# Attention followed by a deformable convolution: two dense taps by spans of rows, and attention scores in float32 by groups of 32 rows

## What is computed

```python
xn = group_norm(x)                                   # 32 groups
q, k, v = split(conv1x1(xn, qkv_w) + qkv_b)          # 4 heads of 32 channels
attn = softmax(q @ k.T * 32 ** -0.5)                 # 4096 x 4096 for each head and image
x = conv1x1(attn @ v, proj_w) + proj_b + x
feat_up = feat_s                                     # the resize keeps the size
om = conv3x3(conv1x1(concat(x, 2 * feat_up), W_off), W_om) + b_om
offset, mask = split(om); mask = sigmoid(mask)       # 8 groups x 9 taps at each pixel
for tap in 9: for group in 8:                        # 16 channels in a group
    val = bilinear(feat_up[group], y + tap_y + off_y, x + tap_x + off_x) * mask
    out += W_dcn[tap, group] @ val
out = relu(out + b_dcn) + x
```

## Time and profile before

| | us |
|---|---|
| median of 3 runs | 12816.8 (12783.6 to 12825.1) |
| the profiled execution | 12790.4 |
| its span | 12788.6 |
| busy in the span: TensorE | 8894 (70%) |
| VectorE | 7910 (62%) |
| ScalarE | 2914 (23%) |
| GpSimd | 10704 (84%) |
| mean granted TensorE clock | 0.819 |

### The profile page before, as it was taken

How to read it: one execution, slowest core, us unless ns; L and a number is a source line. 1 busy time by engine, 2 the same in 40 slices (tenths; PEclk the granted TensorE clock), 3 DMA queues, 4 the chain that set the end, 5 groups by cost and what they waited for, 6 DMA issues and landing times. The chain is left out here.

```text
span 12788.6 us, 126443 instructions
## 1 busy us (share of the span) xinstructions
PE 8894.0 (70%) x34036; PEld 3273.8 (26%) x34036; DVE 7910.4 (62%) x9169; ACT 2914.1 (23%) x3357; POOL 10703.5 (84%) x24581
## 2 busy tenths in 40 slices
PE   5666778765777767777666777766687766778732
PEld 1222222222222222222222222222232222222211
DVE  3466666666666666656666656666566666656633
ACT  2222222211222211222122222211222221222200
POOL 0488888887888888888788888888788888888888
PEclk8888888887888887888788888878788887888865
DMA  3222211112111111111211111111211111111111
GB/s 94 75 65 67 78 29 25 28 29 61 29 32 28 28 28 29 29 29 31 54 35 29 29 27 27 28 28 29 62 24 34 29 28 29 29 29 25 28 24 23
DMA packets 458806, 469.41 MB, mean 37 GB/s; under 512 B 150432, under 2 KB 274464, under 8 KB 458016
## 3 DMA queue, kind: packets, MB, share of 16 engines
q0 software_dynamic: 262144, 268.96, 10.3%
q1 hardware_dynamic: 97952, 119.95, 3.5%
q10 hardware_dynamic: 97920, 71.35, 1.8%
HBM read 390.46 MB, written 69.21 MB: 36 GB/s over the span
## 5 line engine op out<-in xcount | busy, mean ns | idle before, releaser
L408 POOL DMA_INDIRECT g<-patches,idx x8192 | 7862.1, 960 | 1254.6 <-issue 1180.1
L404 POOL TENSOR_TENSOR carrier<-carrier 128x1 f32<-128x1 f32 x15872 | 2766.3, 203 | 140.1
L982 DVE TENSOR_TENSOR ring<-ring,hats 128x1024 f32<-128x1024 f32 x1024 | 1259.3, 1230 | 2520.4 <-PE ring L655 2187.3
L494 ACT ACTIVATE p<-ring 128x1024 f32<-128x1024 f32 x2048 | 2089.2, 1022 | 2812.3 <-PE ring L622 1936.6
L597 PE MATMUL ring<-k,q 128*128 128x512 bf16 x4096 | 1763.9, 529 | 1216.2 <-DVE mx L844 796.3
L844 DVE TENSOR_REDUCE mx<-ring 128x1 f32<-128x1024 f32 x2048 | 2381.1, 1218 | 300.9 <-PE ring L597 300.9
L621 PE MATMUL ring<-q,k 128*128 128x512 bf16 x4096 | 1598.3, 390 | 307.3 <-ACT p L494 84.0
L622 PE MATMUL ring<-q,k 67*128 67x512 bf16 x4096 | 1584.9, 387 | 0.0
L655 PE MATMUL ring<-fx,hats 64*128 64x512 f32 x4096 | 1203.2, 666 | 230.8 <-ACT hats L482 178.8
L984 DVE TENSOR_REDUCE dval<-ring 128x16 f32<-128x1024 f32 x1024 | 1254.1, 1225 | 35.4
L678 PE MATMUL ps_a<-p,v 128*64 128x512 f32 x4096 | 1110.9, 621 | 2.0 <-ACT p L494 2.0
(11 more groups left out here) (117 smaller groups left out, 5707.2 us busy)
## 6 DMA issues: line engine op xcount, KB each, us to landing
g<-patches,idx POOLq DMA_INDIRECT x8192
patch_in<-in_fpad ACTq DMA_DIRECT2D x544, 64.0 KB
patches<-patch_out ACTq DMA_DIRECT2D x136, 256.0 KB
k<-k_parts SPq DMA_DIRECT2D x96, 256.0 KB
q<-q_parts SPq DMA_DIRECT2D x192, 128.0 KB
k_parts<-v SPq DMA_DIRECT2D x16, 768.0 KB
q_parts<-p SPq DMA_DIRECT2D x32, 384.0 KB, 2.6
p<-in_x SPq DMA_DIRECT2D x4, 2048.0 KB
```

Source lines behind the costliest of these rows:

```text
L404: last = nc.gpsimd.tensor_tensor(carrier[:, col:col + 1], carrier[:, 0:1], carrier[:, 0:1], ALU.add)
L408: nc.gpsimd.indirect_dma_start(out=g[:, part, j - CUTS[part] * GROUPS, :], out_offset=None, in_=patches[b], in_offset=bass.IndirectOffsetO ...
L494: nc.scalar.activation(p[:, n % 4, :, :], ring[u % 2][:, :, :], ACT.Exp, scale=SCALE)\
L982: then(V.tensor_tensor(cells, cells, hy[:, at * HEIGHT:(at + 1) * HEIGHT].unsqueeze(2).to_broadcast([128, HEIGHT, GC]), ALU.mult))
```

## The change

- **Scores.** Keys and queries stay float32 in SBUF (`kf`, `qf`, channels on the partitions), written by one ScalarE activation each; `k_parts`, `q_parts`, the splits and all their DMAs go. A head's score is one float32 matmul of 32 rows, at the head's own 32 rows of the array, and in the kt phase one bf16 matmul of 32 rows more, which subtracts the maxima (`ones_b` times `mq`).
- **Max phase.** Still 64 uses of 1024 columns, now two heads x 512 keys: two float32 matmuls of 32 rows on neighbouring row groups. VectorE reduces to two maxima at once.
- **Order in a kt.** Both pairs' float32 matmuls come first, then both pairs' bf16 matmuls, then (in even kt) `distances` and `blocks_of_set`, then `weigh` of the kt before.
- **Two dense taps.** `DENSE` is 2, so 7 taps are picked: 56 picks a tile, in parts of 16, 16, 16 and 8. The 16 dense (tap, group) units of a tile are done in 4 sets of 4. For a set, `distances` has 8 float32 matmuls; ScalarE makes the hats with 4 activations of 512 and 2 of 1024 columns; VectorE multiplies them (`weigh_hats`); `blocks_of_set` has 12 float32 matmuls of 128 rows and 208 columns, for 13 blocks of rows (a span of six rows each, two rows on the partitions, three pairs); VectorE takes the block that holds the pixel (`chosen`) by a multiplication and a sum over 832 results. A set is at kt 0, 2, 4 and 6 of a tile's eight, and its distances two kt earlier.
- `points` gets five more small operations on [128 x 16]. `fx` is loaded by 6 DMAs in place of 2. Sample parts write to their own columns of `g`.

```diff
-DENSE = 1
+DENSE = 2
 PICKED = TAPS - DENSE
-CUTS = tuple(min(2 * part, PICKED) for part in range(PARTS + 1))
+CUTS = tuple(min(2 * part, PICKED - (PARTS - part)) for part in range(PARTS + 1))
...
+SETS = 2 * DENSE
+SET_AT = tuple(i * KT_TILE // SETS for i in range(SETS))
+BLOCK = 5
...
+        def hats_before(t, i):
+            return t * KT_TILE + SET_AT[i - 1] if i > 0 else (t - 1) * KT_TILE + SET_AT[-1]
...
             def prepare(b):
...
-                    nc.scalar.activation(k_made[:, 0, :], ring[u % 2][:, :, :].rearrange("p i n -> p (i n)"), ACT.Identity,
-                                         bias=k_bias).then_inc(k_high, 1)
+                    nc.scalar.activation(kf[:, c * 1024:(c + 1) * 1024], ring[u % 2][:, :, :].rearrange("p i n -> p (i n)"), ACT.Identity,
+                                         bias=k_bias).then_inc(ring_free[u % 2], 1)
...
+            def make_hats(s, b, t, i):
...
+                nc.scalar.activation(made[:, 0, :], ring[k % 2][:, 0, :], ACT.Abs, bias=plus_x, scale=-1.0)
+                for pair in range(PAIRS):
+                    last = nc.scalar.activation(made[:, 1 + pair, :], ring[k % 2][:, 1, :], ACT.Abs, bias=pair_rows[:, pair:pair + 1],
+                                                scale=-1.0)
...
                             for i in range(2):
-                                last = mm(ring[u % 2][:, i, :], q1[:, h, sub * 128:(sub + 1) * 128], k1[:, h, lo:lo + 512],
+                                rows = slice((2 * pair + i) * HD, (2 * pair + i + 1) * HD)
+                                last = mm(ring[u % 2][:, i, :], qf[rows, sub * 128:(sub + 1) * 128], kf[rows, c * 512:(c + 1) * 512],
                                           start=True, stop=True)
...
+            def blocks_of_set(s, b, t, i, fresh):
+                k = set_use(s, t, i)
+                wait_slot_free(pe, before_att(s, b, k), k)
+                pe.wait_ge(hats_weighed, tile_number(s - 1, t) * SETS + i + 1)
...
+                    for pair in range(PAIRS):
+                        last = mm(cells, hats[:, i % 2, 1 + pair, j * 128:(j + 1) * 128], fx[:, pair, :, group * GC:(group + 1) * GC],
+                                  start=pair == 0, stop=pair == PAIRS - 1)
...
+            def scores(s, b, kt, fresh):
...
+                for pair in range(2):
+                    u = uses[pair]
+                    wait_slot_free(pe, before_att(s, b, u), u)
+                    for i in range(2):
+                        rows = slice((2 * pair + i) * HD, (2 * pair + i + 1) * HD)
+                        mm(ring[u % 2][:, i, :], kf[rows, n], qf[rows, :], start=True, stop=False)
+                for pair in range(2):
+                    u = uses[pair]
+                    for i in range(2):
+                        rows = slice((2 * pair + i) * HD, (2 * pair + i + 1) * HD)
+                        last = mm(ring[u % 2][:, i, :], ones_b[rows, :], mq[rows, :], start=False, stop=True)
                     last.then_inc(ring_full, 1)
...
+                for t, i in hats_at(s, kt):
+                    distances(s, b, t, i)
+                for t, i in sets_at(s, kt):
+                    blocks_of_set(s, b, t, i, fresh)
...
             def maxima(s, b, sub0, sub1):
-                        V.tensor_reduce(mx[:, n, c:c + 1], ring[u % 2][:, :, :], AX.XY, ALU.max).then_inc(ring_free[u % 2], 1)
+                        V.tensor_reduce(mx[:, n:n + 2, c], ring[u % 2][:, :, :], AX.X, ALU.max).then_inc(ring_free[u % 2], 1)
```

More of the change, by code:

```diff
@@ L408, in gather @@
                         nc.gpsimd.indirect_dma_start(
[L409 removed]
+                            out=g[:, j, :], out_offset=None, in_=patches[b],
                             in_offset=bass.IndirectOffsetOnAxis(ap=idx[:, t, j:j + 1], axis=0),
@@ new lines, in head @@
+                nc.scalar.activation(qf[:, :], ring[0][:, 0, :], ACT.Identity, bias=q_bias).then_inc(ring_free[0], 1)
+            def make_hats(s, b, t, i):
+                k = hat_use(s, t, i)
+                wait_slot_full(act, before_att(s, b, k), k)
+                made = hats[:, i % 2, :, :]
+                nc.scalar.activation(made[:, 0, :], ring[k % 2][:, 0, :], ACT.Abs, bias=plus_x, scale=-1.0)
+                for pair in range(PAIRS):
+                    last = nc.scalar.activation(made[:, 1 + pair, :], ring[k % 2][:, 1, :], ACT.Abs, bias=pair_rows[:, pair:pair + 1],
+                                                scale=-1.0)
+                last.then_inc(ring_free[k % 2], 1)
+                wait_slot_read(act, before_att(s, b, k), k)
+                for half in range(2):
+                    part = made[:, 2 * half:2 * half + 2, :].rearrange("p v n -> p (v n)")
+                    last = nc.scalar.activation(part, part, ACT.Relu, bias=ones_s[:, 0:1], scale=-1.0)
+                last.then_inc(hats_ready, 1)
@@ L535, in step @@
                     for t in dense_tiles(s):
-                        make_hats(s, b, t)
+                        for i in range(SETS):
+                            make_hats(s, b, t, i)
                         for part in range(PARTS):
@@ L611, in max_to_rows @@
                 for k in range(USE_M):
[L612 removed]
+                    u = max_use(s, k)
                     wait_slot_read(pe, before_att(s, b, u), u)
[L615 to L623 removed]
@@ L657, in columns_of_group @@
                 last.then_inc(ring_full, 1)
             def scores(s, b, kt, fresh):
-                t, j = divmod(kt, KT_TILE)
-                dense = t in dense_tiles(s)
-                if dense and j == 0:
-                    distances(s, b, t)
+                n = slice(kt * 128, (kt + 1) * 128)
+                uses = [score_use(s, kt, pair) for pair in range(2)]
                 for pair in range(2):
-                    scores_of_pair(s, b, kt, pair)
-                    if dense and pair < DENSE:
-                        columns_of_group(s, b, t, j, pair, fresh)
+                    u = uses[pair]
[3 more added lines that the diff above has]
+                        mm(ring[u % 2][:, i, :], kf[rows, n], qf[rows, :], start=True, stop=False)
@@ L756, in step @@
                     for t in dense_tiles(s):
-                        distances(s, b, t)
-                        for j in range(GROUPS):
-                            for d in range(DENSE):
-                                columns_of_group(s, b, t, j, d, fresh)
+                        for i in range(SETS):
+                            distances(s, b, t, i)
+                            blocks_of_set(s, b, t, i, fresh)
                         for part in range(PARTS):
@@ L781, in _ @@
             dve.wait_ge(consts_loaded, CONSTS)
-            V.tensor_scalar(minus_x[:, :], plus_x, -1.0, None, ALU.mult).then_inc(dve_setup, 1)
-            def split(then, src, bias, made, rest):
-                then(V.scalar_tensor_tensor(rest, src, bias, made[:, 0, :], ALU.add, ALU.subtract))
-                then(V.tensor_copy(made[:, 1, :], rest))
-                return V.tensor_sub(made[:, 2, :], rest, made[:, 1, :])
+            for pair in range(PAIRS):
+                V.tensor_scalar(pair_rows[:, pair:pair + 1], base_s[:, 4 * GROUPS:4 * GROUPS + 1], 2.0 * pair, None, ALU.add)
+            V.tensor_scalar(block_rows[:, :].rearrange("p (a b) -> p a b", b=2), steps_s[:, 0:STEPS_B, 0:SUB:2], BLOCK / 4.0, None, ALU.mult)\
+                .then_inc(dve_setup, 1)
+            dve.wait_ge(dve_setup, 2)
             def prepare(b):
@@ L1027, in step @@
                     for t in dense_tiles(s):
-                        for j in range(GROUPS):
-                            dense_group(s, b, t, j)
+                        for i in range(SETS):
+                            weigh_hats(s, b, t, i)
+                            dense_set(s, b, t, i)
                         for part in range(PARTS):
```

303 lines of the change are left out of this document (125 added, 178 removed).

## The result

| | before | after |
|---|---|---|
| median, us | 12820.0 (12783.6 to 12825.1, 4 runs) | 14463.2 (14460.4 to 14467.5, 4 runs) |
| span of the profiled execution | 12788.6 | 14462.1 |
| mean granted TensorE clock | 0.819 | 0.79 |

The ratio is 1.1289 (95% interval 1.1268 to 1.131). Forecast were 13610 us and a range of 12850 to 14600: slower was right and the time lies in the range, but the kernel lost 1643 us where the forecast has 790.

A forecast was written before the change was run, and what follows sets the result against it. GpSimd's picks bound the old kernel; then the TensorE, ScalarE and VectorE chain would, at 362 us plus 54 + 3 - 10 = 47 a step. Start, steps, image changes and tail: 57 + 292 + 1261 + 11452 + 114 + 430 = 13606, predicted 13610 (12850 to 14600).

The forecast's parts named there:

- +3 us for 64 uses: Max phase: a slot's loop gets about 0.05 us a use longer at 2.4 GHz, +3 us a step.
- the max phase stays at 1.2 GHz: Rival, max phase: a use takes 1.9 us in place of 1.2, +45 a step, about 15050 us; chance 0.10.
- From the last maximum to the last `weigh`, +54: Dense part of the kt phase: +49 us a step from kt pairs, +5 from parts of sampling; some 12 is work.
- the copies and the half part: VectorE's small edits: two copies for four, last sampling part with half the patches; put at 0, bounded by 3 us a step.
- The matmuls of four row groups: Kt scores: four float32 matmuls side by side in 0.95 us; with the bf16 ones 1.2 where 1.95 were.
- the set's 4.3 us: Kt phase, `blocks_of_set`: 24 instructions of 208 columns at 0.18 us each, 4.3 us a set.
- the wait ahead of the distances: Even kt: distances take the first pair's slot, free 1.3 us after the scores, following its exponential and a handoff.
- The rival with two row groups side by side: Rival, scores: only two row groups run side by side, 29 us a step more, 14500 us; chance 0.12.
- the faster one: Rival, kt phase: ring waits hidden, dense part adds 12 us a step in place of 54, 12310 us; chance 0.13.
- the waits at the ring: Kt phase: TensorE waits for slots that ScalarE or VectorE still reads; the +54 us a step beyond some 12 of work.
- The queries' trip, -10: Step's start: split queries' trips to HBM go, 11.2 us less 1.5 for the first use, -10 us a step.
- GpSimd's 331 us a step: GpSimd's picks: 224 a step at 1.478 us each, 331 us a step.

The follow-up runs named there:

- e2: Changed kernel with each max-phase matmul on 64 rows in place of 32 (two heads summed, so different maxima): 13599.3 us, ratio 1.062 to the kernel before.
- e3: Changed kernel with 4 block matmuls a set in place of 12, from one pair of rows: 13558.8 us in one run.
- e4: Changed kernel with `weigh` issued ahead of the next kt's distances and blocks: 14745.8 us in one run.
- e8: Changed kernel with zero-padded queries in the max phase, and fewer dense sets a tile in place of 4: three sets 12797.5 us, two sets 12936.7 us.

## Why the forecast fell short

The parts of a step in us, from the traces, for the chain that the forecast starts from (step 8 of before, 361.9 us), and step 14 of after and of e2:

| | before | after | e2 | change forecast | change in after |
|---|---|---|---|---|---|
| step's start to the first maximum | 14.4 | 5.8 | 5.8 | -10 | -9 |
| max phase, first to last maximum | 84.9 | 119.1 | 92.6 | +3 | +34 |
| last maximum to last `weigh` | 203.3 | 249.8 | 249.3 | +54 | +46.5 |
| last `weigh` to the next step | 59.4 | 58.8 | 58.7 | 0 | -1 |

- **The max phase: the step that failed.** The forecast took "+3 us for 64 uses" at 2.4 GHz. Measured are +34 us a step, at 1.71 us a use and 1.2 GHz against 1.16 to 1.18 before. The argument for 2.4 GHz was that TensorE would be busy without a break, from the offset convolution, whose matmuls cover all rows. TensorE was busy 96% and the clock stayed at 0.51. The forecast named the warning under the rival: half of the rows stand idle.
- **By the Trainium skill** ("TensorE: Matmul & The Clock Gate", part 1) the slow clock is the default and activity releases it. The forecast read activity as busy time. The runs say that with float32 matmuls on 32 of 128 rows, two at a time, busy time is not enough (0.51), and with 64 rows each the clock is 0.94.
- **The right rival** was "the max phase stays at 1.2 GHz", given 0.10. Its first reason, "it does so now", holds for the 16 us of the earlier trace rows and not for the phase (0.65 above); the second, the idle rows, is the one that e2 shows. It was priced at 15050 us from a use of 1.9 us, twice a stream of 0.95; at half the clock it is 1.71. With that, 0.51 over the forecast's use, it gives 13606 + 32 x 64 x 0.51 = 14650, with +36 us a step for the max phase where +34 are measured. The rest of the 190 us is mostly in the next bullet. What the clock alone is worth is less than 0.51 a use: in e2 a use takes 1.29 us on average, not 1.20, and the phase is 8 us longer than before and not 3.
- **From the last maximum to the last `weigh`, +54.** Measured are +46.5. From the first exponential on, 186.5 us became 241.0. Ahead of it, 16.8 us became 8.8: the first distances no longer stand there (6 us at a tile's start), two copies of the maxima take 0.42 us each where four took 2.50, and the part of sampling is half. The forecast put the copies and the half part at 0. The matmuls of four row groups, the set's 4.3 us and the wait ahead of the distances (1.18 us for 1.3) came as forecast. That the hats would be ready long before their use did not always hold: the blocks wait 139 us in all for `weigh_hats`. The rival with two row groups side by side (0.12) is out. So is the faster one: e3 and e4 show that the waits at the ring are real.
- **The queries' trip, -10.** Measured are -9.
- **The sum.** Start 52 for 57. Step 0: 330 for 292; e2 has 301, so 30 of these 38 are the clock's. Steps 1 to 3: 1374 for 1261; e2 has 1294, so 81 of 113. Steps 4 to 30: 11817 us where 27 x 409 + 114 = 11157 were forecast, 660 more, 27 x 24.4. Step 31 and the tail: 889 for 839. Together +856. In e2, with the clock put right, the same five terms are off by -7, +9, +33, -60 and +22. They add up to -3, so its match with the forecast is luck in part.
- **GpSimd's 331 us a step** were not the bound in after, as forecast, but they were too low: (14451.6 - 377.6 - 2854.1) / 7168 = 1.565 us a pick, 351 a step, reckoned as in the forecast from the rows of tile g. With fewer sets (e8) it mattered.

## What to carry to other kernels

Before small matmuls replace large ones, look at how many of the array's rows are fed at one time: a phase of them can stay at 1.2 GHz however busy it is (119 us here where 93 were possible). If rows stand idle anyway, feeding them zeros can be worth it (764 us here for four small activations a step). When an engine that was the bound gets work taken away, look first at what the others still do one after another at the phase borders; here three positions of 5.3 us stood on the path, and moving them, 12 us a step, made the difference between no gain and 2.6%.

## What the runs showed of the hardware that I had not expected

**The clock goes by more than TensorE's busy share.** Float32 matmuls of 512 columns in the max phase: 32 rows each on two row groups, busy 117 of 122 us, 0.51; 64 rows each, busy 79 of 95 us, 0.94; 64 rows each with half of the stationary rows zero, 77 of 95 us, 0.94. All 128 rows don't suffice by themselves either: with the bf16 matmuls of before, TensorE was busy 14.01 of 16 us at 0.50 in one window, and 61 of 86 us at 0.65 over a whole max phase. What tells these from the float32 matmuls on all rows no run shows.

**GpSimd's small operations stop during one VectorE operation.** L973 (`weigh_hats`) is a multiplication with both inputs and the output in SBUF. GpSimd's and VectorE's timelines in the run with two sets:

```profile
4410.02 0.34 POOL L404 TENSOR_TENSOR carrier<-carrier 128x1 f32<-128x1 f32 x2
...
4411.50 1.90 POOL L404 TENSOR_TENSOR carrier<-carrier 128x1 f32<-128x1 f32 x2
```

```profile
4411.60 1.75 DVE L973 TENSOR_TENSOR hats<-hats 128x1536 f32<-128x1536 f32 x1
```

Two additions of one column take 0.34 us, and 1.90 us when L973 starts beside them; they end as it ends. The operation between two picks has a mean of 221 ns here and 203 in the kernel before, 15872 times: 3045 us of busy time in place of 2766, 279 more. Of the 243 that took over 0.5 us, 241 ended within 0.2 us of the end of an L973 (in after all 324 within 0.33 us of its like, L959). These 279 us are most of the 8192 x 0.040 = 328 us that the picks cost over the 1.478 us forecast. By the Trainium skill ("SBUF — State Buffer", section on who interferes with whom) a `tensor_tensor` with both inputs in SBUF keeps GpSimd's reads of SBUF out until it ends; the rows agree.
